# Self-attention of one transformer block: a new step order for units 1 to 14, with small shifts per engine

## The chip, the cores and the metric

One NeuronCore of a Trainium2 chip runs the whole program in a single launch. The metric is device time in microseconds, the median of several runs. Three runs of the kernel before gave 1282.04 us as median (1281.49 to 1285.37).

## What is computed

The input `x` is (2, 1024, 256) in float32. The block adds self-attention, cross-attention, a gated feed-forward and a ternary-weight feed-forward with quantised activations. The change touches the self-attention alone:

```python
h1 = adaln(x, t, norm1_w, norm1_b)
x = mha(h1, h1, attn1_wq, attn1_wk, attn1_wv, attn1_wo, attn1_bo) + x     # 16 heads of 64, 1024 queries and keys
h2 = adaln(x, t, norm2_w, norm2_b)
x = mha(h2, context, attn2_wq, ...) + x                                   # 77 keys
# mha: softmax(q k^T / 8) v per head, then @ wo + bo
```

Matrix products run as sums of fp16 parts: each operand is split into a high part and a low remainder.

## The kernel before, in words

**Units.** Self-attention is done in 16 units (g = 0 to 15), each two heads of one batch. A unit has 16 chunks (c = 0 to 15): head (c // 8), half of the queries (c // 4 % 2), and a group of 256 keys (c % 4). Python code builds one list of steps (`Schedule.attention`, `unit`, `extras`), and each engine gets the same list, from which it runs its own part. The order of the list is therefore the order of work on every engine, except for small shifts (`program`): a step kind may be moved some places up or down on one engine. Before the change such shifts hold for cross-attention only.

**Steps**, with the short names that this document uses:

- S c, `scores` (L797 to L814): four matmuls of 512 columns into one of two PSUM buffers. ACT takes the exponential of the chunk (L1116) into a ring of four SBUF buffers. S c waits until the exponential of chunk c-2 is done.
- R c, `rest`: the low remainder of the exponentials, on Pool (L1406), or on DVE (L1640) for chunks 0, 5 and 11 (`rest_on_pool`, L106).
- V c, `values` (L816 to L839): 24 matmuls of 65 or 64 columns, which need R c. After every fourth chunk DVE divides by the sum (L1651, L1653).
- M, `max`: one matmul of 512 columns (L774) and a DVE maximum over it (L1617). They are numbered by head, tile and key half (M160 is head 1, tile 6, half 0), 32 for a unit, in two PSUM banks by turns, so an M waits for the DVE maximum of the M two places before. The last of each head (M071, M171) also makes the head's negated maximum (L1628). All 16 of head 0 and the first 8 of head 1 are run in the unit before.
- row0, row1: PE transposes the negated maxima of a head (L783), ACT copies them (L1098) and starts a 2 KB DMA from its own queue (L1100) into the operand buffer. S 0 waits for the DMA of row0, S 8 for that of row1.
- q0, q1, k0, k1: projections for the next unit (L753, six matmuls), then ACT (L1087), then DVE (L1602). After k1 the SP queue starts six DMAs (`restack`, L620) that bring them to the layout of the next unit, 1.5 MB in all. The first M of the next unit, M000, waits for the first three.
- v0, v1: value projections (L763, 24 matmuls), ACT (L1091), DVE (L1609).
- out0, out1: transposes of the finished half heads (L787), then ACT (L1106) and DVE (L1633).
- P, `proj`: output projection of an older unit (L730, 12 matmuls), then DVE (L1662). N, `normT`: transposes of normalised tokens (L716), then two DVE operations (L1592). Units 1 to 3 have two N each, units 4 to 7 and 12 to 14 two P, units 8 to 11 two P (with statistics, L1507 and L1511) and two N. Below they are the early, the plain and the double units.

q, k, v, out, P and N share one PSUM bank, so each of them waits on PE until DVE has read the one before (`st.after`):

```python
            def piece(st):
                if st.after:
                    pe.wait_ge(*consumed(st.after))
```

**What sets the order.** In `unit` a loop over the chunks puts S c+1, R c, half of that chunk's other steps, V c-1, the other half, and then `extras` (P and N). Every engine executes its own instructions strictly in the order written, each after its semaphore waits.

## Time and profile before

| | |
|---|---|
| median of three runs | 1282.04 us |
| the profiled execution, its own time | 1283.78 us |
| its span | 1282.0 us |
| PE busy | 1132.9 us (88%) |
| DVE busy | 893.1 us (70%) |
| Pool busy | 640.2 us (50%) |
| ACT busy | 595.1 us (46%) |
| mean granted PE clock | 0.965 |
| share of the chain that ended last | PE 58%, DVE 17%, DMA 9%, issue 5%, ACT 4% |
| start of unit 1's S 1 to start of unit 15's S 1 | 115.44 to 790.40 us |

A busy time is the sum of an engine's instructions. Matmuls overlap in the pipeline (a 512-column matmul lasts 0.38 us and the next starts 0.22 us later), so PE at 88% says little on its own. The time of a step on PE is read from starts, and a wait is where two starts lie further apart than usual.

### The profile page before, as it was taken

To read this page: it belongs to the slowest core of one execution; us is meant where nothing else is said; L and a number is where in the kernel's file an instruction comes from. 1 tells how busy PE (TensorE), PEld (TensorE's weight loads), DVE (VectorE), ACT (ScalarE), POOL (GpSimd) and SP (SyncE) were. 2 spreads that over 40 slices of the span, in tenths; PEclk is the share of its full clock that TensorE was granted. 3 is DMA by queue.
4 is the path that set the end of the run, shared out by engine and by line. 5 is a ranking of instruction groups with operands and counts; after the bars stand their busy time and mean duration, and the time that the engine had idled before them with its cause. 6 is when DMAs were issued, how large, how long until landed. Compare 5 with 4: busy or idle time off the path is not lost.

```text
span 1282.0 us, 30609 instructions
## 1 busy us (share of the span) xinstructions
PE 1132.9 (88%) x12739; PEld 736.9 (57%) x12739; DVE 893.1 (70%) x1754; ACT 595.1 (46%) x855; POOL 640.2 (50%) x572
## 2 busy tenths in 40 slices
PE   4789999999999999899889998988998799799876
PEld 1245655665665665565556655666676566365554
DVE  5668867766766767767757668578688656765764
ACT  3334545444444444444444455445444442465655
POOL 6646755655555555655645555356356343511220
PEclk7799999999999999999999999999999999999987
DMA  7330220121021021020120222134333520000000
GB/s 268 80 85 2 51 51 12 40 51 35 18 51 37 16 51 29 23 51 9 43 51 2 51 51 67 28 81 120 81 70 66 150 85 1 1 5 13 17 2 33
DMA packets 41854, 63.52 MB, mean 50 GB/s; under 512 B 11459, under 2 KB 22383, under 8 KB 41461
## 3 DMA queue, kind: packets, MB, share of 16 engines
q1 hardware_dynamic: 40413, 60.91, 19.0%
q8 instruction: 101, 1.65, 0.5%
q10 hardware_dynamic: 1304, 0.66, 0.2%
q14 instruction: 36, 0.29, 0.1%
HBM read 20.63 MB, written 2.10 MB: 18 GB/s over the span
## 4 chain that ended last, share of the span: by engine, by line
PE 58%; DVE 17%; DMA 9%; issue 5%; ACT 4%; POOL 3%; SPq 3%; DVEq 0%; ACTq 0%
PE outs L753 8%; PE mixed L774 6%; PE scores L812 6%; PE scores L813 6%; DMA head_operands<-qk_pairs 4%; PE scores L871 4%; PE outs L730 4%; PE outs L835 4%; PE outs L837 4%; PE outs L836 3%; DVE maxes L1617 3%; SPq L620 3%; PE outs L887 3%; DMA head_operands<-neg_max_rows 2%; PE outs L763 2%
## 5 line engine op out<-in xcount | busy, mean ns | idle before, releaser
L1406 POOL TENSOR_TENSOR exps_rest<-exps 128x1024 f16<-128x1024 f32 (+1 forms) x267 | 465.2, 1748 | 343.1 <-ACT exps L1116 342.2
L1116 ACT ACTIVATE exps<-scores 128x1024 f32<-128x1024 f32 (+1 forms) x320 | 298.2, 937 | 237.7 <-PE scores L813 226.6
L1617 DVE TENSOR_REDUCE maxes<-mixed 128x1 f32<-128x512 f32 x512 | 335.6, 683 | 62.0 <-PE mixed L774 59.6
L835 PE MATMUL outs<-values,exps 128*128 128x65 f16 (+1 forms) x2176 | 228.4, 193 | 7.3 <-POOL exps_rest L1406 6.8
L812 PE MATMUL scores<-head_operands 128*128 128x512 f16 (+1 forms) x576 | 219.9, 382 | 15.2 <-DMA head_operands<-neg_max_rows 14.8
L836 PE MATMUL outs<-values,exps 128*128 128x64 f16 (+1 forms) x2176 | 228.4, 192 | 0.0
L837 PE MATMUL outs<-values,exps_rest 128*128 128x65 f16 (+1 forms) x2176 | 228.2, 194 | 0.0
L835 PEld LDWEIGHTS outs<-values,exps 128*128 128x128 bf16 (+1 forms) x2176 | 201.7, 98 | 36.0 <-POOL exps_rest L1406 11.1
L813 PE MATMUL scores<-head_operands 128*128 128x512 f16 (+1 forms) x576 | 219.4, 381 | 0.0
L836 PEld LDWEIGHTS outs<-values,exps 128*128 128x128 bf16 (+1 forms) x2176 | 200.8, 98 | 25.9 <-issue 0.3
L774 PE MATMUL mixed<-head_operands 128*128 128x512 f16 x512 | 180.8, 388 | 25.9 <-DMA head_operands<-qk_pairs 11.7
L837 PEld LDWEIGHTS outs<-values,exps_rest 128*128 128x128 f16 (+1 forms) x2176 | 200.8, 97 | 0.0
L753 PE MATMUL outs<-hT,weights 128*128 128x512 f16 x492 | 124.4, 391 | 4.2 <-DVE qk_pairs L1602 1.8
L1602 DVE SCALAR_TENSOR_TENSOR qk_pairs<-outs,qk_pairs 128x512 f16<-128x512 f32 x82 | 56.4, 688 | 94.9 <-ACT qk_pairs L1087 94.9
L774 PEld LDWEIGHTS mixed<-head_operands 128*128 128x128 f16 x512 | 49.9, 98 | 88.0 <-DVE maxes L1617 28.4
L1087 ACT ACTIVATE qk_pairs<-outs 128x512 f16<-128x512 f32 x82 | 49.0, 597 | 105.5 <-PE outs L753 105.5
L812 PEld LDWEIGHTS scores<-head_operands 128*128 128x128 f16 (+1 forms) x576 | 57.8, 100 | 58.7 <-issue 16.9
L730 PE MATMUL outs<-weights,attn_outT 128*128 128x256 f16 x744 | 91.2, 273 | 0.0
L871 PE MATMUL scores<-hT,weights 128*128 128x512 f16 x384 | 90.0, 387 | 1.3 <-DVE exps L1700 1.3
L813 PEld LDWEIGHTS scores<-head_operands 128*128 128x128 f16 (+1 forms) x576 | 58.1, 101 | 50.0 <-issue 1.4
L753 PEld LDWEIGHTS outs<-hT,weights 128*128 128x128 f16 x492 | 44.7, 100 | 57.3 <-DVE attn_outT L1633 9.8
L730 PEld LDWEIGHTS outs<-weights,attn_outT 128*128 128x128 f16 x744 | 70.6, 98 | 11.1
...
## 6 DMA issues: line engine op xcount, KB each, us to landing
head_operands<-qk_pairs SPq DMA_DIRECT2D x128, 256.0 KB, 4.1
...
```

Of the source, the lines that this page charges most:

```text
L730: last = mm(ITEM[bank][:, 0:D], OT[:, c, xh, t * P:(t + 1) * P], W[:, 3, wh, c * D:(c + 1) * D], start=(n_ == 0 and c == 4 * half), stop=( ...
L753: last = mm(m[:, 0:rhs.shape[-1]], W[:, 0 if kind == "q" else 1, wh, wc[c]], rhs, start=(n_ == 0 and c == 0), stop=(n_ == 2 and c == KC - 1))
L774: last = mm(m[:, :], hb[:, QS, t * P:(t + 1) * P], hb[:, KH, kh * HALF:(kh + 1) * HALF], start=True, stop=True)
L812: mm(o, kb[:, KH, :], hb[:, QS, :], start=True, stop=False)
L813: last = mm(o, kb[:, KL, :], hb[:, QM, :], start=False, stop=True)
L835: mm(o, eb[:, sl], vb[:, DH:VW], start=(kt == 0 and q == 0), stop=False, skip_group_check=True)
L836: mm(o[:, 0:DH], eb[:, sl], vb[:, 0:DH], start=False, stop=False, skip_group_check=True)
L837: last = mm(o, R[0:a.ks, slot, sl], vb[:, DH:VW], start=False, stop=(kt == a.kt - 1), skip_group_check=True)
L871: last = mm(SP_[f % 2][:, half * HALF:(half + 1) * HALF], WU[:, wh, k, half * F + f * P:half * F + (f + 1) * P], hT[:, xh, k, tc * HALF:(t ...
L1116: A(E[0:a.ks, c % RING, 0:n], SP_[c % 2][0:a.ks, 0:n], ACT.Exp, scale=SCALE).then_inc(s.exps, 1)
L1406: G.tensor_tensor(R[0:a.ks, c % RING, 0:n], e, e.bitcast(BF16).rearrange("p (n two) -> p n two", two=2)[:, :, 1], ALU.subtract).then_inc(s ...
L1617: V.tensor_reduce(mx[:, h, t, kh:kh + 1], m[:, :], AX_X, ALU.max).then_inc(s.maxed, 1)
```

## The change

Units 1 to 14 no longer come from the loop but from a written table, `SELF_UNIT`. It holds the same steps as before; only their places differ. Units 0 and 15 keep the loop. Besides, `program` now applies shifts in self-attention too, units 0 and 15 included: on Pool P moves 5 steps down and the bias addition 2 up; on ACT the exponentials move 1 up and row 1 down; on DVE the remainders (R) move 4 up. Which remainders run on DVE stays (0, 5, 11).

```diff
+SELF_UNIT = (
+    ("scores", 1), ("rest", 0), ("max", 0, 1, 8), ("max", 0, 1, 9), ("q", 1, 0), ("max", 0, 1, 10), ("slot", 0),
...
+SELF_LAGS = {"POOL": {"proj": 5, "norm": -2},
+             "ACT": {"scores": -1, "row": 1},
+             "DVE": {"rest": -4}}
+SELF_RESTS = (0, 5, 11)
...
-            return c not in (0, 5, 11) if g < UNITS - 1 else bool(c % 2)
+            return c not in SELF_RESTS if g < UNITS - 1 else bool(c % 2)
...
+    def self_unit(self, a, g):
+
+        stage = g // 4
+        pieces = {0: ("norm1", "normT1", "hi1", "lo1"), 2: ("projB", "norm", "normT", "hi", "lo")}.get(stage, ("projA",))
+        for kind, *at in SELF_UNIT:
+            if kind in ("scores", "rest", "values"):
+                self.add(kind, 0, g + at[0] // a.chunks, c=at[0] % a.chunks)
+            elif kind == "slot":
+                self.notes(g, at[0])
+            elif kind in ("q", "k", "v", "row", "out", "max"):
+                what = (kind, at[1]) if kind != "max" else ("max", at[1], at[2] // 2, at[2] % 2)
+                self.add("item", 0, g + at[0], what)
+            elif kind in pieces:
...
         for g in range(UNITS):
-            self.unit(a, g, slots if g else first)
+            if g in (0, UNITS - 1):
+                self.unit(a, g, slots if g else first)
+            else:
+                self.self_unit(a, g)
...
-        lags = LAGS.get(engine, {})
-        at = self.cross_at
+        lags = SELF_LAGS.get(engine, {}), LAGS.get(engine, {})
+        at = self.self_at, self.cross_at
...
-            return i + (lags.get(kind, 0) if i >= at else 0)
+            return i + (lags[1].get(kind, 0) if i >= at[1] else lags[0].get(kind, 0) if i >= at[0] else 0)
```

The order on PE in a plain unit, before and after, in short names (what changed place is easiest seen around V, M and S):

```
before: S1 M M q0 S2 M V0 q1 S3 M M V1 k0 S4 M V2 k1 S5 M V3 M S6 row1 V4 v0 S7 M000 V5 M S8 M M V6 v1 S9 M M V7 M
        S10 M V8 M P S11 M M V9 M S12 M V10 M P S13 M V11 M S14 M row0 V12 M S15 M M V13 out0 S0 M V14 M V15 M M out1
after:  S1 M M q0 M S2 V0 q1 S3 M V1 k0 M S4 M k1 V2 S5 S6 M M S7 V3 row1 v0 V4 V5 M000 M V6 S8 M M v1 S9 M M V7 P M
        S10 M V8 M S11 M M V9 M S12 M P M V10 M V11 S13 M S14 M row0 V12 M S15 V13 M M out0 S0 M V14 M V15 M M out1
```

**DVE at the boundary of two units**, from the division after V 15 to q0's part. L1617 is M, L1633 out1, L1640 R 0, L1602 q0. Before:

```order
L1651 RECIPROCAL rden<-outs 128x4
L1653 TENSOR_TENSOR attn_out<-outs,rden 128x4x64
L1617 TENSOR_REDUCE maxes<-mixed 128x1 x2
L1633 TENSOR_TENSOR attn_outT<-outs,attn_outT 128x512
L1640 TENSOR_TENSOR exps_rest<-exps 128x1024
L1617 TENSOR_REDUCE maxes<-mixed 128x1 x2
L1602 SCALAR_TENSOR_TENSOR qk_pairs<-outs,qk_pairs 128x512
```

The same place after the change (L1670 is M, L1686 out1, L1693 R 0, L1655 q0):

```order
L1704 RECIPROCAL rden<-outs 128x4
L1706 TENSOR_TENSOR attn_out<-outs,rden 128x4x64
L1670 TENSOR_REDUCE maxes<-mixed 128x1
L1693 TENSOR_TENSOR exps_rest<-exps 128x1024
L1670 TENSOR_REDUCE maxes<-mixed 128x1
L1686 TENSOR_TENSOR attn_outT<-outs,attn_outT 128x512
L1670 TENSOR_REDUCE maxes<-mixed 128x1 x2
L1655 SCALAR_TENSOR_TENSOR qk_pairs<-outs,qk_pairs 128x512
```

R 0 has moved ahead of the last M of this group (M131) and of out1.

**DVE around row1**, from k1's part (L1602, L1655) to v0's (L1609, L1662). L1628 and L1681 make the negated maximum that row1 needs. Before:

```order
L1602 SCALAR_TENSOR_TENSOR qk_pairs<-outs,qk_pairs 128x512
L1617 TENSOR_REDUCE maxes<-mixed 128x1
L1651 RECIPROCAL rden<-outs 128x4
L1653 TENSOR_TENSOR attn_out<-outs,rden 128x4x64
L1617 TENSOR_REDUCE maxes<-mixed 128x1
L1628 TENSOR_REDUCE neg_max<-maxes 128x8
L1640 TENSOR_TENSOR exps_rest<-exps 128x1024
L1609 SCALAR_TENSOR_TENSOR values<-outs,values 128x8x64
```

After:

```order
L1655 SCALAR_TENSOR_TENSOR qk_pairs<-outs,qk_pairs 128x512
L1693 TENSOR_TENSOR exps_rest<-exps 128x1024
L1670 TENSOR_REDUCE maxes<-mixed 128x1 x2
L1681 TENSOR_REDUCE neg_max<-maxes 128x8
L1704 RECIPROCAL rden<-outs 128x4
L1706 TENSOR_TENSOR attn_out<-outs,rden 128x4x64
L1662 SCALAR_TENSOR_TENSOR values<-outs,values 128x8x64
```

R 5 now stands ahead of both last maxima (M170, M171) and of the negated maximum; before it stood behind them.

**PE from k0 to k1.** L753 and L806 are the projections, L812 and L813 (L865 and L866) S 4, L774 (L827) an M; where lines are left out stand the 24 matmuls of V 2. Before:

```order
L753 MATMUL outs<-hT,weights 128x512 x6
L812 MATMUL scores<-head_operands 128x512
L813 MATMUL scores<-head_operands 128x512
L812 MATMUL scores<-head_operands 128x512
L813 MATMUL scores<-head_operands 128x512
L774 MATMUL mixed<-head_operands 128x512
...
L753 MATMUL outs<-hT,weights 128x512 x6
```

After:

```order
L806 MATMUL outs<-hT,weights 128x512 x6
L827 MATMUL mixed<-head_operands 128x512
L865 MATMUL scores<-head_operands 128x512
L866 MATMUL scores<-head_operands 128x512
L865 MATMUL scores<-head_operands 128x512
L866 MATMUL scores<-head_operands 128x512
L827 MATMUL mixed<-head_operands 128x512
L806 MATMUL outs<-hT,weights 128x512 x6
```

V 2 has left the space between k0 and k1; it follows k1 now, and an M came in.

## Rows read from the trace of the kernel before

**Rows 1.** Windows, unit 5: span, busy of PE, PEld, DVE, ACT, Pool, PE clock

```profile
300.46:347.70 47.24, 45.08 (x588) 29.28 (x586) 32.26 (x56) 21.46 (x26) 25.28 (x13) 1.00 0.16 35
```

**Rows 2.** Waits of PE, 115.44 to 790.40: total us, times, longest

```profile
PE mixed L783 <- DVE neg_max L1628: 13.0, 24, 1.5
PE mixed L774 <- DMA head_operands<-qk_pairs: 11.0, 11, 2.1
PE scores L812 <- DMA head_operands<-neg_max_rows: 5.9, 4, 1.8
PE outs L835 <- POOL exps_rest L1406: 5.6, 12, 0.6
```

**Rows 3.** Timeline of PE in unit 6: start us, duration us, instruction

```profile
357.87 0.38 PE L774 MATMUL mixed<-head_operands 128*128 128x512 f16 x1
358.09 0.19 PE L835 MATMUL outs<-values,exps 128*128 128x65 f16 x1
358.82 1.46 PE L753 MATMUL outs<-hT,weights 128*128 128x512 f16 x6
360.11 0.38 PE L812 MATMUL scores<-head_operands 128*128 128x512 f16 x1
```

**Rows 4.** Timeline of DVE in unit 6 around k1 and row1

```profile
360.94 0.69 DVE L1602 SCALAR_TENSOR_TENSOR qk_pairs<-outs,qk_pairs 128x512 f16<-128x512 f32 x1 [1.81 <-ACT qk_pairs L1087]
...
362.69 0.68 DVE L1617 TENSOR_REDUCE maxes<-mixed 128x1 f32<-128x512 f32 x1
363.48 0.17 DVE L1628 TENSOR_REDUCE neg_max<-maxes 128x8 f32<-128x16 f32 x1
```

**Rows 5.** Timeline of ACT in unit 6: S 5's exponential, row1

```profile
361.18 1.02 ACT L1116 ACTIVATE exps<-scores 128x1024 f32<-128x1024 f32 x1 [0.27 <-PE scores L813]
...
364.12 0.25 ACT L1098 ACTIVATE neg_max_rows<-mixed 8x128 f16<-8x128 f32 x1
```

**Rows 6.** Timeline of DVE at the boundary of units 5 and 6

```profile
347.01 1.28 DVE L1617 TENSOR_REDUCE maxes<-mixed 128x1 f32<-128x512 f32 x2
348.53 0.69 DVE L1633 TENSOR_TENSOR attn_outT<-outs,attn_outT 128x512 f16<-128x512 f32 x1 [0.25 <-ACT attn_outT L1106]
349.14 1.21 DVE L1640 TENSOR_TENSOR exps_rest<-exps 128x1024 f16<-128x1024 f32 x1
350.27 1.28 DVE L1617 TENSOR_REDUCE maxes<-mixed 128x1 f32<-128x512 f32 x2
```

**Rows 7.** Chain that ended last, at q0 of unit 6: start us, us, what

```profile
349.28 0.39 PE outs L753
```

**Rows 8.** Chain that ended last, units 6 and 7: the restack's DMA

```profile
362.94 5.88 DMA head_operands<-qk_pairs
368.82 0.14 issue
...
411.50 4.75 DMA head_operands<-qk_pairs
```

**Rows 9.** Unit 8: k1's part on DVE (timeline), row1's DMA (chain)

```profile
456.91 0.69 DVE L1602 SCALAR_TENSOR_TENSOR qk_pairs<-outs,qk_pairs 128x512 f16<-128x512 f32 x1 [1.81 <-ACT qk_pairs L1087]
...
461.68 4.40 DMA head_operands<-neg_max_rows
```

**Rows 10.** Timeline of PE in unit 6: M071 and row0

```profile
386.62 0.38 PE L774 MATMUL mixed<-head_operands 128*128 128x512 f16 x1
...
388.48 0.27 PE L783 MATMUL mixed<-identf,neg_max 128*8 128x128 f32 x1 [0.41 <-DVE neg_max L1628]
```

**Rows 11.** Timeline of DVE in unit 8: N, M, P with statistics, R 11

```profile
473.36 0.72 DVE L1592 TENSOR_SCALAR h_full<-outs,norm_cols 128x128 f32<-128x128 f32 x2
...
475.73 0.42 DVE L1662 SCALAR_TENSOR_TENSOR residual<-outs,residual 128x256 f32<-128x256 f32 x1 [0.46 <-PE outs L730]
...
476.81 1.29 DVE L1617 TENSOR_REDUCE maxes<-mixed 128x1 f32<-128x512 f32 x2
...
478.61 2.07 DVE L1640 TENSOR_TENSOR exps_rest<-exps 128x1024 f16<-128x1024 f32 x1
```

More of the change, by code:

```diff
@@ L54 @@
 Q_HI, Q_LO, K_HI, K_LO = range(4)
+SELF_UNIT = (
+    ("scores", 1), ("rest", 0), ("max", 0, 1, 8), ("max", 0, 1, 9), ("q", 1, 0), ("max", 0, 1, 10), ("slot", 0),
+    ("rest", 1), ("scores", 2), ("rest", 2), ("values", 0), ("q", 1, 1), ("scores", 3), ("max", 0, 1, 11),
+    ("slot", 1), ("slot", 2), ("slot", 3), ("values", 1), ("k", 1, 0), ("max", 0, 1, 12), ("scores", 4),
+    ("rest", 3), ("max", 0, 1, 13), ("k", 1, 1), ("values", 2), ("scores", 5), ("scores", 6), ("rest", 4),
+    ("rest", 5), ("max", 0, 1, 14), ("norm1", 0), ("max", 0, 1, 15), ("projB", 0), ("scores", 7), ("rest", 6),
+    ("values", 3), ("row", 0, 1), ("v", 1, 0), ("slot", 4), ("slot", 5), ("values", 4), ("values", 5),
+    ("max", 1, 0, 0), ("max", 1, 0, 1), ("normT1", 0), ("slot", 6), ("values", 6), ("scores", 8), ("rest", 7),
+    ("max", 1, 0, 2), ("norm", 0), ("hi1", 0), ("max", 1, 0, 3), ("v", 1, 1), ("scores", 9), ("rest", 8),
+    ("max", 1, 0, 4), ("max", 1, 0, 5), ("values", 7), ("projA", 0), ("normT", 0), ("slot", 7),
+    ("max", 1, 0, 6), ("slot", 8), ("lo1", 0), ("norm1", 1), ("hi", 0), ("scores", 10), ("max", 1, 0, 7),
+    ("values", 8), ("rest", 9), ("lo", 0), ("max", 1, 0, 8), ("scores", 11), ("rest", 10), ("max", 1, 0, 9),
+    ("hi1", 1), ("max", 1, 0, 10), ("projB", 1), ("slot", 9), ("values", 9), ("normT1", 1), ("max", 1, 0, 11),
+    ("scores", 12), ("slot", 10), ("rest", 11), ("max", 1, 0, 12), ("projA", 1), ("max", 1, 0, 13),
+    ("slot", 11), ("lo1", 1), ("values", 10), ("norm", 1), ("max", 1, 0, 14), ("rest", 12), ("values", 11),
+    ("normT", 1), ("scores", 13), ("hi", 1), ("slot", 12), ("max", 1, 0, 15), ("scores", 14), ("slot", 13),
+    ("rest", 13), ("max", 1, 1, 0), ("row", 1, 0), ("values", 12), ("max", 1, 1, 1), ("lo", 1), ("rest", 14),
+    ("scores", 15), ("values", 13), ("rest", 15), ("max", 1, 1, 2), ("max", 1, 1, 3), ("slot", 14),
+    ("out", 0, 0), ("scores", 16), ("max", 1, 1, 4), ("values", 14), ("max", 1, 1, 5), ("values", 15),
+    ("max", 1, 1, 6), ("max", 1, 1, 7), ("slot", 15), ("out", 0, 1), ("slot", 16))
+SELF_LAGS = {"POOL": {"proj": 5, "norm": -2},
+             "ACT": {"scores": -1, "row": 1},
+             "DVE": {"rest": -4}}
+SELF_RESTS = (0, 5, 11)
 CROSS_UNIT = (
@@ L170, in extras @@
                             self.norm(kind, NT + tile + t)
-            if (g, c) in ((0, 2), (1, 2)):
-                self.add("setup", what="tokens8" if g == 0 else "tokens12")
-            if g == 1 and c in (2, 4, 6, 8):
-                self.add("split_low", what=c // 2 - 1, c=3)
-            if (g, c) in ((14, 8), (14, 11), (15, 1)):
-                self.add("split", c={8: 4, 11: 5, 1: 6}[c])
+            self.notes(g, c)
             if late:
@@ L179, in extras, with notes @@
                     self.add("item", 1, v, what)
+    def notes(self, g, c):
+        if (g, c) in ((0, 2), (1, 2)):
+            self.add("setup", what="tokens8" if g == 0 else "tokens12")
+        if g == 1 and c in (2, 4, 6, 8):
+            self.add("split_low", what=c // 2 - 1, c=3)
+        if (g, c) in ((14, 8), (14, 11), (15, 1)):
+            self.add("split", c={8: 4, 11: 5, 1: 6}[c])
+    def self_unit(self, a, g):
[10 more added lines that the diff above has]
+            elif kind in pieces:
+                tile = 2 * (g % 4) + at[0]
+                if kind[:4] == "proj":
+                    self.proj(0, g // 8 if kind == "projA" else 0, int(kind == "projB"), tile)
+                elif stage == 0:
+                    self.norm(kind if kind == "norm1" else kind[:-1], TPB + tile)
+                else:
+                    self.norm(kind, NT + tile)
     def cross_unit(self, a, g, first_max):
```

2 lines of the change are left out of this document (added).

## The prediction, made before the changed kernel was run

> **What bounds the kernel now.** I read the table first, then the windows of single units, then PE's waits over units 1 to 14, and last the timelines of PE, DVE and ACT around each wait. Unit 5 takes 47.24 us at full clock, and PE is busy for 45.08 of them, DVE for 32.26, ACT for 21.46 and Pool for 25.28 [rows 1]. PE sets the pace, and only where it waits is there anything to win or lose. The waits view names four reasons [rows 2]: the negated maxima for row0 and row1 (13.0 us), the restack's DMA before M000 (11.0), row1's DMA before S 8 (5.9), and remainders on Pool (5.6). An order that lost all four would win 35.5 us.
>
> Steps on PE, from starts [rows 3]: M 0.22, V 0.73 (358.09 to 358.82), q or k 1.29, S (four matmuls like M's) 0.86, v 1.3 (24 matmuls of a quarter of 512 columns), P 1.3 (12 of half), N 0.2, row 0.1. A result is visible 0.21 after its PE step: the exponential of S 5 starts 1.07 after S 5 [rows 3, 5], and 1.07 less 0.86 is 0.21. On DVE an M follows an M after 0.60 (1.28 less 0.68), an operation that follows R starts 1.13 after R's start [rows 6], and the negated maximum is ready 0.96 after the start of its last M [rows 4], for PE 0.14 later [rows 8].
>
> **The change, wait by wait.** No instruction is added or removed, so the price is only in waits.
>
> *q0, all 14 units: +11.3.* At the unit's boundary DVE starts M130 at 347.01 and M131 at 347.61, ends out1's part at 349.22, and q0, which needs the bank, starts at 349.28 [rows 6, 7]. Now R 0 stands between the two M. Its exponential is ready in time: S 0 starts 0.86 + 0.22 + 0.73 + 0.22 + 0.73 = 2.76 before M130's matmul and needs 1.07 + 1.02. So R 0 starts at 347.61, M131 at 348.74, out1's part at 349.34, which ends at 350.03, and q0 starts at 350.09: 0.81 later. In the old place R 0 stood behind out1, where PE waited for nothing of it. If DVE had slack there the cost would be 0; at most it is the whole 1.13.
>
> *k1, 14 units: +3.9.* k1 needs k0's bank. From start to free a projection takes 2.87 (358.82 to 360.94, 0.69, and 0.06 as at q0) [rows 3, 4, 7]. Between them PE now has k0, M, S, M = 2.59, without V 2's 0.73. It waits 0.28. Before it did not wait.
>
> *row1, early and plain units: +4.4.* Count from S 5's start. Its exponential ends at 2.09, R 5 starts at 2.15 and now stands ahead of M170: M170 3.28, M171 3.88, negated maximum 4.84, row1 at 4.98. PE arrives after S 5, S 6, M, M, S 7, V 3 = 3.75 and waits 1.23. Before, the maximum ended at 363.65 [rows 4] and row1 could go at 363.79, while PE had finished S 6 at 360.11 + 0.86 + 0.22 + 0.73 + 0.22 + 0.86 = 363.00, so it waited 0.79. That is +0.44 in each of ten units. In the double units a P of 1.3 covers both.
>
> *M000: -10.4.* In the new order k1 starts 2.02 before S 5, its DVE part ends 2.81 after its start, so at +0.79. In unit 6 the first three DMAs were there 7.3 us after this point, in unit 7 6.2 (1.3 to the third issue, 5.88 or 4.75, 0.14) [rows 8]. PE now arrives at M000 after row1's 4.98 + 0.1 + 1.3 (v0) + 1.46 (V 4, V 5) = 7.84, which is 7.05 after it. The 11.0 us of [rows 2] go; of the long kind (three units) 0.2 stays each.
>
> *S 8: +2.9.* What is late next is row1's own DMA, since R 5 has delayed row1 and V 6 is all that came between. ACT copies it from 5.31 to 5.56 (0.33 after row1, 0.25 long) [rows 5], that is 4.8 after k1's part. In unit 8 the copy was done at 461.66, 4.1 after k1's part (457.60), and the row was there at 466.22: 4.54 after the copy, 8.6 after k1's part [rows 9]. PE arrives at S 8 at 7.84 + 0.44 + 0.73 = 9.01, or 8.2 after k1's part. If the row lands no earlier than in unit 8 the wait is 0.4, if it again takes 4.54 it is 1.1. I take 0.6, nearer to the first, because by then the restack's six DMAs are nearly through. In the double units ACT first does S 7's exponential, which needs V 3 (end 5.06); the copy ends at 6.55, 5.8 after k1's part, PE arrives at 8.3: 0.3 to 2.0, taken as 0.7. Ten times 0.6 and four times 0.7 is 8.8, and the 5.9 of [rows 2] go.
>
> The Trainium skill (DMA: Bandwidth & Descriptors, Queues, rings and completion order) says that a DMA engine goes round its queues packet by packet, so a 2 KB row would not stand behind 1.5 MB. By it S 8 would not wait at all; the trace's 4.40 us for such a row [rows 9] speaks against it. It is a rival below.
>
> *row0: -4.0.* Before, a division stood ahead of M071, and row0 came 1.86 after M071's matmul [rows 10] with 1.30 of work between: 0.56 of waiting. Now S 13 stands between V 11 and M071, so row0 can go 0.22 + 0.21 + 0.96 + 0.14 = 1.53 after it, a wait of 0.23. That is 0.33 in ten units, and I take half of it in the double ones, where N mixes in.
>
> *M061, early units: +4.3.* R 11 and N now stand ahead of M051 on DVE. From S 11's start: R 11 starts at 2.49 (behind M041 at 1.29 and M050 at 1.89), N at 3.62, M051 at 4.25 (N takes 0.63 [rows 11]); its bank is free at 4.99. PE arrives at M061 after S, M, M, V, N, M, S, M = 3.55 and waits 1.44, in three units. *Double units: +4.5.* There P's DVE part (1.08 from 475.73 to 476.81 [rows 11]) starts at 2.8, R 11 at 3.9, M051 at 5.0, free at 5.77; PE arrives at 4.64 and waits 1.13, in four units. In the plain units P's 1.3 lies between and covers it.
>
> *Remainders on Pool: -4.0.* The twelve waits of 5.6 us are three in each double unit [rows 2]. Pool now does R 10 ahead of P's statistics (shift 5), and the first two should go; the third, before V 15, behind N's part, I leave at 0.4. Bounds: -5.6 and 0.
>
> At no cost: the shift of ACT's exponentials (exponentials and rows keep their turns except ahead of row1, counted above), the 2 up of Pool's bias additions (nobody waits for them [rows 2]), and units 0 and 15, where R moves ahead of q1 and P on DVE: an exponential is ready 2.1 after its S, before those are. If that cover fails, eight R of 1.13 in unit 15 cost some 3 us; if V 8 to V 10 come sooner, they win 1.
>
> In unit 8 an R on DVE took 2.07 instead of 1.21 while Pool did its own [rows 6, 11]. The Trainium skill (SBUF — State Buffer, Who interferes with whom) explains it: a DVE instruction with two SBUF inputs and a Pool instruction share a port that is held for a whole instruction. By it R 0 and R 5 at their new places cost nothing more, as Pool's R 15 and R 4 end before them; were one caught, each catch would add up to 0.9.
>
> **Sum.** 11.3 + 3.9 + 4.4 - 10.4 + 2.9 - 4.0 + 4.3 + 4.5 - 4.0 = +12.9 us. The profiled execution took 1283.78 us, 1.74 above the median of the runs, so 1296.7 for its like and 1295 for the median.
>
> **Rivals.**
> - *The rows of maxima wait for the whole restack (slower still).* Then S 8 waits 1.1 and 2.0: 10 x 0.5 + 4 x 1.3 = +10, 1305 us. For it: the 4.54 of unit 8. Against: the traffic is older when the row is issued.
> - *The rows slip in between (near no change).* S 8 never waits: -8.8, 1286 us. For it: only four units ever waited there. Against: [rows 9].
> - *The moved remainders cost nothing (faster).* DVE is idle for 15 us of a unit [rows 1]. If R 0, R 5 and R 11 fell into such gaps, q0, row1 and both M061 terms were nil: 12.9 - 11.3 - 4.4 - 4.3 - 4.5 = -11.6, 1270 us. It decides at one place: whether DVE starts out1's part as soon as ACT has done its own. Against: DVE takes its work in written order, and around M130 it has no gap [rows 6].
>
> **How the numbers follow.** Forecast 0.58 (its own range 1288 to 1302), rows late 0.14, rows early 0.13, remainders free 0.15. A measurement of this kernel can tell about 0.3% (3.8 us) from no change, so faster is under 1278.2 and slower over 1285.9. Faster 0.13 is nearly all of the last case. Same 0.13 is the rest of it and most of the rows-early case. Slower 0.74 is what is left. The range 1276 to 1307 takes the rows-late case in and cuts off most of the free remainders; the long DMAs, which fell in three units, can fall in none or in six (some 4 us), and lie inside it.
>
> **What would show it.** In the changed profile PE's wait for out1's DVE part before q0 should be near 1.1 in each unit (0.3 before), M000 should hardly wait, row1 should wait for L1681 by about 1.2 with R 5 on DVE just before M170, S 8 should wait for the row's DMA in nearly every unit, and M061 in seven. A plain unit should last 47.24 + 0.81 + 0.28 + 0.44 - 0.8 + 0.6 - 0.33, about 48.2. I am wrong if a plain unit lasts less than 47.2, or if DVE runs R 0 without delaying out1.

## The result and the profile after

| | before | changed |
|---|---|---|
| median, us (runs) | 1284.96 (13) | 1292.91 (13) |
| lowest to highest | 1276.72 to 1292.38 | 1287.65 to 1299.83 |
| profiled execution, its span | 1283.78, 1282.0 | 1299.83, 1298.0 |
| S 1 of unit 1 to S 1 of unit 15 | 674.96 | 684.47 |
| unit 15 | 46.81 | 43.18 |

The changed kernel takes 1.0069 times as long, 95% interval 1.0043 to 1.0096, or +8.9 us (5.5 to 12.3); the two medians lie 8.0 us apart. The forecast was 1295 us, slower. The profiled execution of the changed kernel is the longest of its 13, so its whole span overstates the change. Its start (66.25 us to S 1 of unit 0, 61.28 before) and what follows unit 15 (448.9 after 444.8) account for that. The kernels below all leave both alone, and there the two ranged from 60.7 to 66.9 and from 440.5 to 446.6. So I compare the units.

The head of the page after:

```profile
span 1298.0 us, 30602 instructions
PE 1138.3 (88%) x12732; PEld 739.2 (57%) x12739; DVE 890.8 (69%) x1754; ACT 594.4 (46%) x855; POOL 626.5 (48%) x572
```

Windows of the changed kernel, unit 5 (the answer to [rows 1]) and unit 15 (span, busy PE, PEld, DVE, ACT, Pool, clock):

```profile
313.03:360.93 47.90, 45.23 (x589) 29.44 (x587) 32.47 (x56) 21.46 (x26) 24.65 (x13) 1.00 0.15 35
805.92:849.10 43.18, 38.81 (x547) 25.80 (x545) 26.93 (x44) 21.72 (x28) 16.33 (x8) 0.99 0.19 39
```

The plain unit is 0.66 longer with the same work on every engine, so only waits can have changed. Unit 15 of the kernel before:

```profile
790.40:837.21 46.81, 39.47 (x547) 26.10 (x545) 28.40 (x44) 21.74 (x28) 16.99 (x8) 0.96 0.16 34
```

Its clock differs too: the mean granted clock of unit 15 was 0.96 before and 0.99 after.

PE's waits in the changed kernel over the middle units, 121.46 to 805.92 (total us, times, longest), against [rows 2]:

```profile
PE mixed L827 <- DVE maxes L1670: 16.8, 24, 1.7
PE mixed L836 <- DVE neg_max L1681: 11.6, 11, 1.1
PE scores L865 <- DMA head_operands<-neg_max_rows: 8.3, 11, 2.0
...
PE outs L806 <- DVE attn_outT L1686: 2.9, 14, 0.2
PE outs L888 <- POOL exps_rest L1459: 1.3, 4, 0.3
...
PE mixed L827 <- DMA head_operands<-qk_pairs: 0.2, 1, 0.2
```

M000's wait is gone (11.0 to 0.2), eight of the twelve on Pool too (5.6 to 1.3). New are 16.8 us in which an M waits for a DVE maximum. All but three of the 24 stand at two places, M141 and M061.

At the boundary of a unit, DVE and then PE (start us, us, instruction), against [rows 6, 7]:

```profile
360.23 0.68 DVE L1670 TENSOR_REDUCE maxes<-mixed 128x1 f32<-128x512 f32 x1
360.83 1.22 DVE L1693 TENSOR_TENSOR exps_rest<-exps 128x1024 f16<-128x1024 f32 x1
361.96 0.69 DVE L1670 TENSOR_REDUCE maxes<-mixed 128x1 f32<-128x512 f32 x1
362.56 0.68 DVE L1686 TENSOR_TENSOR attn_outT<-outs,attn_outT 128x512 f16<-128x512 f32 x1
```

```profile
362.70 0.39 PE L827 MATMUL mixed<-head_operands 128*128 128x512 f16 x1 [0.54 <-DVE maxes L1670]
363.30 0.39 PE L806 MATMUL outs<-hT,weights 128*128 128x512 f16 x1 [0.21 <-DVE attn_outT L1686]
```

R 0 stands between M130's maximum and M131's, and from M130's maximum to q0 it is 3.07 us, where it was 2.27. The wait is split: 0.70 of it falls on M141, which needs M131's bank, and 0.38 on q0 (0.28 before).

In a double unit, behind P's DVE part and R 11:

```profile
491.02 0.42 DVE L1715 SCALAR_TENSOR_TENSOR residual<-outs,residual 128x256 f32<-128x256 f32 x1 [0.24 <-PE outs L783]
...
492.04 1.19 DVE L1693 TENSOR_TENSOR exps_rest<-exps 128x1024 f16<-128x1024 f32 x1
493.15 1.28 DVE L1670 TENSOR_REDUCE maxes<-mixed 128x1 f32<-128x512 f32 x2
```

```profile
493.90 0.39 PE L827 MATMUL mixed<-head_operands 128*128 128x512 f16 x1 [0.89 <-DVE maxes L1670]
```

The chain that ended last, from S 5 to S 8 of unit 6 (start us, us, what), against [rows 4, 5, 9]:

```profile
375.50 1.03 ACT exps L1169
376.55 1.23 DVE exps_rest L1693
377.78 1.21 DVE maxes L1670 x2
...
379.08 0.18 DVE neg_max L1681
379.26 0.14 issue
379.40 0.28 PE mixed L836
...
380.00 3.71 DMA head_operands<-neg_max_rows
383.71 0.14 issue
383.84 0.38 PE scores L865
```

R 5 delays the last two maxima of head 1, these delay row1, and the row's DMA then ends PE's wait at S 8.

**The terms.** For each step of PE I took the time to the next start and subtracted the usual pace of that step, the same in both kernels (S 0.861 us, V 0.730, q and k 1.292, v 1.337, P 1.308, out 0.436, N 0.217, M 0.215, row 0.107). What is left is waiting, or time at a lower granted clock. Summed over units 1 to 14, us:

| wait at | forecast change | before | after | change |
|---|---|---|---|---|
| q0, and M141 ahead of it | +11.3 | 4.0 | 15.2 | +11.2 |
| k1 | +3.9 | 0 | 4.9 | +4.9 |
| row1 | +4.4 | 8.8 | 12.2 | +3.4 |
| M000 | -10.4 | 13.6 | 0.6 | -13.0 |
| S 8 | +2.9 | 4.7 | 10.6 | +5.9 |
| row0 | -4.0 | 8.1 | 4.4 | -3.7 |
| M061 | +8.8 | 0.1 | 8.9 | +8.8 |
| V 10, V 12 (Pool) | -4.0 | 5.1 | 0.4 | -4.8 |
| all others | 0 | 21.0 | 17.8 | -3.2 |
| sum | +12.9 | 65.4 | 75.0 | +9.6 |

The middle stretch itself grew by 9.5, so the waits account for all of it: without them a plain unit takes 44.09 before and 44.05 after. In "all others" the largest changes are S 0 (-2.4, nearly all one wait of the kernel before in unit 11), M030 (-1.5), M070 and V 9 (-0.6 each), and against them M040 (+1.0) and M041 (+0.7). With unit 15's -3.6 and unit 0's +1.0 (54.16 to 55.20) the change up to the end of unit 15 is +6.9; the medians differ by 8.0.

Each kernel also lost some 1.7 us to the clock once, right behind PE's longest wait of this stretch. In the changed kernel S 8 of unit 10 waited 2.20, and from 581.97 to 585.39 the granted clock was 0.50 (1.2 GHz; the same columns as above):

```profile
581.97:585.39 3.42, 3.42 (x25) 2.60 (x24) 1.61 (x3) 1.02 (x1) 1.30 (x2) 0.50 0.00 0
```

In it v1 took 2.40 us instead of 1.34. In the kernel before M000 of unit 12 waited 2.24, and the clock was 0.50 from 665.52 to 668.93. So what looks like a wait behind v1 in unit 10 is PE at work at the lower level.

### The profile page after: what moved, and what is told of

Same layout as the page of the kernel before. It is cut to its first block, busy times and chain, and to the rows that moved or that the text cites. A ratio compares the mean times of both kernels' runs of the same rounds, so it can differ in the third digit from the quotient of the medians.

```text
span 1298.0 us, 30602 instructions
## 1 busy us (share of the span) xinstructions
PE 1138.3 (88%) x12732; PEld 739.2 (57%) x12739; DVE 890.8 (69%) x1754; ACT 594.4 (46%) x855; POOL 626.5 (48%) x572
## 4 chain that ended last, share of the span: by engine, by line
PE 56%; DVE 21%; DMA 7%; issue 5%; ACT 5%; POOL 3%; SPq 3%; DVEq 0%; ACTq 0%
PE outs L806 8%; PE scores L865 6%; PE scores L866 6%; PE mixed L827 5%; DVE maxes L1670 5%; DMA head_operands<-neg_max_rows 4%; PE scores L924 4%; PE outs L783 4%; PE outs L890 3%; PE outs L888 3%; PE outs L889 3%; DVE exps_rest L1693 3%; SPq L673 3%; PE outs L940 2%; PE outs L816 2%
## 5 line engine op out<-in xcount | busy, mean ns | idle before, releaser
L1459 POOL TENSOR_TENSOR exps_rest<-exps 128x1024 f16<-128x1024 f32 (+1 forms) x267 | 456.5, 1716 | 369.9 <-ACT exps L1169 369.8
L1670 DVE TENSOR_REDUCE maxes<-mixed 128x1 f32<-128x512 f32 x512 | 336.5, 685 | 77.4 <-PE mixed L827 73.9
L865 PE MATMUL scores<-head_operands 128*128 128x512 f16 (+1 forms) x576 | 220.4, 383 | 20.8 <-DMA head_operands<-neg_max_rows 17.5
L866 PE MATMUL scores<-head_operands 128*128 128x512 f16 (+1 forms) x576 | 220.4, 383 | 0.0
L827 PE MATMUL mixed<-head_operands 128*128 128x512 f16 x512 | 181.8, 390 | 28.4 <-DVE maxes L1670 22.7
L806 PE MATMUL outs<-hT,weights 128*128 128x512 f16 x492 | 125.4, 393 | 8.5 <-DVE attn_outT L1686 4.0
L1655 DVE SCALAR_TENSOR_TENSOR qk_pairs<-outs,qk_pairs 128x512 f16<-128x512 f32 x82 | 56.6, 691 | 103.5 <-ACT qk_pairs L1140 103.5
L827 PEld LDWEIGHTS mixed<-head_operands 128*128 128x128 f16 x512 | 48.0, 98 | 88.9 <-DVE maxes L1670 48.7
L865 PEld LDWEIGHTS scores<-head_operands 128*128 128x128 f16 (+1 forms) x576 | 57.9, 101 | 68.7 <-issue 19.5
L866 PEld LDWEIGHTS scores<-head_operands 128*128 128x128 f16 (+1 forms) x576 | 58.2, 101 | 49.4 <-issue 1.2
L806 PEld LDWEIGHTS outs<-hT,weights 128*128 128x128 f16 x492 | 44.8, 100 | 67.1 <-DVE qk_pairs L1655 12.4
L1693 DVE TENSOR_TENSOR exps_rest<-exps 128x1024 f16<-128x1024 f32 x53 | 65.2, 1230 | 25.0 <-ACT exps L1169 25.0
```

The source lines that it names most:

```text
L806: last = mm(m[:, 0:rhs.shape[-1]], W[:, 0 if kind == "q" else 1, wh, wc[c]], rhs, start=(n_ == 0 and c == 0), stop=(n_ == 2 and c == KC - 1))
L827: last = mm(m[:, :], hb[:, QS, t * P:(t + 1) * P], hb[:, KH, kh * HALF:(kh + 1) * HALF], start=True, stop=True)
L865: mm(o, kb[:, KH, :], hb[:, QS, :], start=True, stop=False)
L866: last = mm(o, kb[:, KL, :], hb[:, QM, :], start=False, stop=True)
L1459: G.tensor_tensor(R[0:a.ks, c % RING, 0:n], e, e.bitcast(BF16).rearrange("p (n two) -> p n two", two=2)[:, :, 1], ALU.subtract).then_inc(s ...
L1670: V.tensor_reduce(mx[:, h, t, kh:kh + 1], m[:, :], AX_X, ALU.max).then_inc(s.maxed, 1)
```

## The experiments

Each is one edit. "Plain unit" is unit 5 or the span over units 4 to 7, in the kernel's profiled execution. Unless said otherwise the edit is to the changed kernel, and ratios are to the kernel before.

### 1. R 0 back behind out1

```diff
 # in place(): DVE's R 0 of units 1 to 14 gets no shift
+            if engine == "DVE" and kind == "rest" and st.ai == 0 and st.c == 0 and 0 < st.g < UNITS - 1:
+                return i
```

> The changed kernel, but R 0 of units 1 to 14 keeps its old place on DVE, behind out1 and ahead of M140. Theory (remainders ahead of maxima on DVE make PE wait): PE's waits before M141 and q0, 0.70 and 0.40 in the changed kernel, shrink to the 0.3 before q0 of the kernel before, so a unit is 0.8 us shorter (a plain unit 47.1 instead of 47.9) and the program about 11 us faster than the changed kernel, 0.2% faster than the kernel before. Rival (the loss is in the order of PE's steps and the DMA of the row of maxima, whatever DVE does): R 0 moves nothing, a plain unit stays at 47.9.

Measured: 1286.49 us, ratio 1.0016 (0.9993 to 1.0040), against the changed kernel's 1.0069 (1.0043 to 1.0096). Plain unit 47.50 to 47.58 (unit 7 48.14). M141's 0.70 is gone and q0 is back at 0.28, as the term says. But another wait has come, on PE behind q0 (start us, us, instruction):

```profile
361.29 1.47 PE L808 MATMUL outs<-hT,weights 128*128 128x512 f16 x6
363.02 0.39 PE L829 MATMUL mixed<-head_operands 128*128 128x512 f16 x1 [0.26 <-DVE maxes L1672]
```

This is M150. In the new order it follows q0 at once, and it needs the bank of M140, whose maximum DVE reaches only after R 0, at 362.28. It waits 0.44 against the pace, so of the 0.80 a unit only 0.36 is won. In the kernel before no M waited behind q0, with R 0 in this same place.

### 2 and 3. The shifts alone, and the order alone

```diff
 # 2: old order, new shifts
-            if g in (0, UNITS - 1):
-                self.unit(a, g, slots if g else first)
-            else:
-                self.self_unit(a, g)
+            self.unit(a, g, slots if g else first)
```

> The old order of steps in all units, with the new shifts per engine (R 4 up on DVE, P 5 down and bias 2 up on Pool, exponentials 1 up and row 1 down on ACT). Theory: R 0 ahead of M131 costs 0.8 before q0, R 5 ahead of the last maximum costs row1 1.2 of which M000's wait of 0.8 swallows a part, R 11 ahead of M051 costs M061 0.4: some 1.9 us per unit, 1310 us (+2%). Rival (the shifts are harmless, the written order is what costs): within 0.3% of the kernel before.

```diff
 # 3: new order, no shifts
+SELF_LAGS = {}
```

> The new order of steps with all shifts of self-attention at zero. Theory: the waits before M141 and q0 shrink by 0.8 in 14 units, those before M061 (1.4 in three early units, 1.05 in four double ones) go, since R 11 is behind M051 again; row1's 1.2 stays, since the table itself puts R 5 ahead of M170; the waits on Pool's remainders in the double units come back in part. About 18 us faster than the changed kernel, 1275 us, 0.8% faster than the kernel before. Rival (order costs, shifts harmless): as slow as the changed kernel, about 1293.

Measured: the shifts alone 1299.09 us, ratio 1.0136 (1.0096 to 1.0176); the order alone 1286.19 us, 1.0021 (1.0003 to 1.0039). So most of the loss comes with the shifts. That it is DVE's remainders among them is read from the waits of these kernels and from experiments 1 and 4; no run moves DVE's alone. The shifts alone had been expected to take 1310; but M000's wait, 13.6 before, fell to 0.8, and unit 15 became 4.2 shorter. In the old order the shifts cost more than in the new: with R 5 ahead of the last maximum row1 waits 2.03 a unit (23.3 us over the fourteen, 12.2 in the changed kernel), which the waits of that kernel show (total us, times, longest):

```profile
PE mixed L833 <- DVE neg_max L1678: 26.5, 28, 2.3
PE scores L862 <- DMA head_operands<-neg_max_rows: 8.9, 9, 1.5
PE mixed L824 <- DVE maxes L1667: 8.1, 16, 0.5
```

Without shifts row1 still waits 12.2, since the table itself puts R 5 ahead of M170: that term comes with the order. And three wins that I had counted on stayed away (1275 expected). R 0 back in its place makes M150 wait 0.44, as in experiment 1, 6.2 us in all. R 11, back in its place, no longer delays M061 (but for 0.36 in the early units) but M070 behind it (5.1 us in all, 0.70 in a double unit):

```profile
486.75 0.39 PE L825 MATMUL mixed<-head_operands 128*128 128x512 f16 x1 [0.54 <-DVE maxes L1668]
```

And unit 15 took 46.77 there, 42.64 with the shifts alone: what makes unit 15 shorter is the shift, not the order. DVE in unit 15 of the kernel before, then Pool:

```profile
795.61 2.29 DVE L1500 SCALAR_TENSOR_TENSOR weights<-stage,weights 128x2048 f16<-128x2048 f32 x1 [0.77 <-ACT weights L1044]
797.82 2.92 DVE L1640 TENSOR_TENSOR exps_rest<-exps 128x1024 f16<-128x1024 f32 x1
```

```profile
796.83 2.83 POOL L1406 TENSOR_TENSOR exps_rest<-exps 128x1024 f16<-128x1024 f32 x1 [2.02 <-ACT exps L1116]
```

And DVE in unit 15 of the changed kernel:

```profile
810.05 1.23 DVE L1693 TENSOR_TENSOR exps_rest<-exps 128x1024 f16<-128x1024 f32 x1
811.84 2.29 DVE L1553 SCALAR_TENSOR_TENSOR weights<-stage,weights 128x2048 f16<-128x2048 f32 x1 [0.57 <-ACT weights L1097]
```

R 2 stood behind the split of a weight (2.29 us) and beside Pool's R 3, where it took 2.92, and the maxima behind it let PE wait 2.38 at M161:

```profile
801.40 0.39 PE L774 MATMUL mixed<-head_operands 128*128 128x512 f16 x1 [2.38 <-DVE maxes L1617]
```

Four places up it is ahead of the split, alone, and takes 1.23: the remainder ends 5.13 after the split's start before, and 0.56 ahead of it now. Besides, the granted clock of the kernel before was 0.50 for 3.41 us from 802.05, right behind that wait, and q1 took 2.54 us from 802.60 instead of 1.29: part of the 3.6 is the clock.

### 4. All remainders of units 0 to 14 on Pool

```diff
-SELF_RESTS = (0, 5, 11)
+SELF_RESTS = ()
```

> The changed kernel with the remainders 0, 5 and 11 of units 0 to 14 on Pool too, none on DVE (SELF_RESTS empty). Theory: the waits before M141 and q0 fall to 0.3, row1's 1.2 to about 0.1, those before M061 go; row1's copy on ACT then stands behind the exponential of S 7, so S 8 waits for the row's DMA by about 1.5 instead of 0.6. A plain unit 46.3, the program about 20 us faster than the changed kernel, near 1273. Rival (Pool becomes the bound: 16 remainders of 1.9 are 30 us of a unit of 47, and in the double units and early units Pool has 4 to 8 us more): V 1, V 6 and V 12 wait for Pool by over 1 us each and nothing is won.

Measured: 1266.51 us, ratio 0.9879 (0.9848 to 0.9911). Plain unit 46.9 to 47.0 (unit 7 47.8). M141's wait is gone, row1's is 0.1, M061's is 0.36 in the early units only. Pool, busy for 30.1 of a unit's 46.9, isn't late anywhere new. With the divided remainders out of the way, most of what PE still waits for is row1's DMA (total us, times, longest; the next line is out1's wait for the division, which all kernels have):

```profile
PE scores L865 <- DMA head_operands<-neg_max_rows: 14.5, 13, 1.9
PE outs L840 <- DVE attn_out L1706: 5.4, 14, 0.4
PE mixed L827 <- DMA head_operands<-qk_pairs: 2.9, 4, 1.3
```

This confirms the three terms that rest on a remainder on DVE: over the fourteen units q0 with M141 fell by 11.2, row1 by 11.2 and M061 by 7.8. Of these 30.2 us S 8 took 6.0 back and M000, which PE now reaches earlier, 3.6. So S 8 isn't late only because row1 is: the copy now ends 4.39 after k1's part instead of 4.75, and S 8 still goes no sooner than 8.5 after it, so that PE, which is there earlier, waits longer (1.2 to 1.5 in the plain units, 2.05 once).

### 5. R 5 behind the negated maximum

```diff
 # in place(): DVE's R 5 of units 1 to 14 goes behind M171 and its negated maximum
+            if engine == "DVE" and kind == "rest" and st.ai == 0 and st.c == 5 and 0 < st.g < UNITS - 1:
+                return i + (3.5 if st.g < 4 else 2.5)
```

> The changed kernel, but R 5 of units 1 to 14 stands on DVE behind M171 and its negated maximum instead of ahead of M170. Theory: row1's wait of 1.2 in ten units falls to about 0.1; its copy on ACT then stands behind the exponential of S 7, so the copy comes only 0.4 earlier against k1 and S 8's wait grows from 0.5 to about 1.4. Net 0.3 to 0.4 less for a plain unit (47.5 instead of 47.9), nothing in the double ones; the program 3 us faster than the changed kernel, within its noise. Rival (what follows row1 is not late, so removing its wait pays in full): a plain unit 46.7, the program 11 us faster.

Measured: 1290.58 us, ratio 1.0038 (1.0014 to 1.0063). Plain unit 47.75 to 47.8 (unit 7 48.6). The time is near what I expected for another reason. Row1's wait went, and S 8's nearly so (10.6 to 3.0 over the fourteen units); what took their place is V 4, which needs the division after V 3 (12.3 us in the early and plain units), and in the double units v0, which waits 1.1 to 1.3 for P's part on DVE (5.1 us in all). DVE, and PE at V 4:

```profile
374.96 0.17 DVE L1683 TENSOR_REDUCE neg_max<-maxes 128x8 f32<-128x16 f32 x1
375.04 2.43 DVE L1695 TENSOR_TENSOR exps_rest<-exps 128x1024 f16<-128x1024 f32 x1
377.39 0.17 DVE L1706 RECIPROCAL rden<-outs 128x4 f32<-128x4 f32 x1
377.60 0.42 DVE L1708 TENSOR_TENSOR attn_out<-outs,rden 128x256 f32<-128x256 f32 x1
```

```profile
378.17 0.19 PE L890 MATMUL outs<-values,exps 128*128 128x65 f16 x1 [1.29 <-DVE attn_out L1708]
```

Pool did its own remainders at that time:

```profile
374.50 4.73 POOL L1461 TENSOR_TENSOR exps_rest<-exps 128x1024 f16<-128x1024 f32 x2 [2.42 <-ACT exps L1171]
```

R 5 took 2.43 where it took 1.23 at its place in the changed kernel. In each such pair of these traces it is the operation that started second that was lengthened: R 5 here, R 2 in unit 15 before, and Pool's R 1 in experiment 1 (2.24, behind an R 0 of 1.21). The Trainium skill (SBUF — State Buffer, Who interferes with whom) tells of a port that such a DVE instruction and a Pool instruction hold by turns; the trace agrees as far as it goes: 2.43, 2.92 and [rows 11] 2.07 where one of Pool's remainders had started before, 1.19 to 1.23 where DVE was alone or first. No run here takes Pool's alone away at one of these places.

### 6. Head 1's restack behind row1's DMA

All remainders on Pool as in 4, and in units 1 to 14 SP issues the second three DMAs of the restack only when row1 of the unit has landed:

```diff
+                    if ai == 0 and h == 1 and 1 < g:
+                        sp.wait_ge(s.rows[1], 16 * g + CREDIT)
```

> The kernel with all remainders on Pool, and in restack the three DMAs of the second head (h = 1) wait until row1's DMA of the unit before has landed (SP waits for rows[1]; units 2 to 15). Theory (the 2 KB row is late because 1.5 MB of restack is on the same DMA engines): the row lands some 2.7 us after its copy instead of 4.2, S 8's wait of 1.2 to 1.5 falls to under 0.3 in 13 units, nobody waits for the second head's operands (needed 17 us later); 15 us faster than the kernel with all remainders on Pool, 1251. Rival (the row's time is its own latency, whatever else moves, as packet-wise turns between queues would have it): S 8 waits as before, 1266.

Measured: 1248.04 us, ratio 0.9707 (0.9664 to 0.9751), 18.5 us under 4. Plain unit 45.51, a window of it:

```profile
292.76:338.28 45.52, 44.82 (x589) 29.35 (x587) 29.38 (x53) 21.36 (x26) 30.14 (x16) 1.00 0.17 37
```

S 8 waits once in the fourteen units (0.9, in unit 10). When row1's copy ends on ACT and when the restack of head 1 starts, which needs the row there:

```profile
355.91 0.25 ACT L1153 ACTIVATE neg_max_rows<-mixed 8x128 f16<-8x128 f32 x1
```

```profile
357.87 1.95 SPq L675 DMA_DIRECT2D head_operands<-qk_pairs  x3
```

From the end of the copy, 356.16, to 357.87 are 1.71 us, the most that the row can have taken, for the same 2 KB that took 3.71 in the changed kernel. The DMA packets say where the time went. Here head 0's packets had ended at 357.09, and the row's ran alone, from 357.47 to 357.55. In unit 6 of the changed kernel they ran from 382.22 to 382.83, in the midst of the restack's, and the row landed another 0.88 later. So what makes the row late is the restack's traffic, not the DMA's own time.

### 7. Row1 ahead of the exponential of S 7

All remainders on Pool, and on ACT:

```diff
+            if engine == "ACT" and kind == "scores" and st.ai == 0 and st.c == 7 and 0 < st.g < UNITS - 1:
+                return i + 3.5
+            if engine == "ACT" and st.ai == 0 and st.what == ("row", 1) and 0 < st.g < UNITS - 1:
+                return i
```

> The kernel with all remainders on Pool, and on ACT row1's copy and DMA stand ahead of the exponential of S 7 in units 1 to 14. Theory: the copy ends 0.8 earlier (0.8 to 0.9 in the double units), but under the restack's traffic the row lands only 0.3 to 0.8 earlier; S 8 waits 0.4 to 0.8 less, 6 to 10 us faster than the kernel with all remainders on Pool, about 1259. Rival (S 8's release is set by the end of the restack, 8.6 us after k1's part, whenever the row is issued): no change, 1266.

Measured: 1255.39 us, ratio 0.9759 (0.9720 to 0.9797), 11.1 under 4. Plain unit 45.8 to 46.8, S 8's waits fell from 16.6 to 4.3. The row's copy ends 3.64 after k1's part instead of 4.39, and in four of the seven plain units S 8 goes 7.4 to 7.5 after it, with hardly a wait. In units 5 and 7 it still waits 1.1.

### 8. The old order with all remainders on Pool

The edits of 2 and 4 together.

> The old order of steps in all units, with the new shifts, and no remainders of units 0 to 14 on DVE. It tells whether the 18 us that the kernel with all remainders on Pool wins over the kernel before come from the new order or from the division. Theory (the remainders at their old places on DVE cost nothing, the new order wins once they are gone): plain units as before, 47.2, unit 15 shorter by 3.6 as in the changed kernel; about 1280. Rival (the division alone wins): 1266.

Measured: 1275.02 us, ratio 0.9917 (0.9884 to 0.9951). The old order keeps row1's 0.80, M000's 0.8 to 2.1 and row0's 0.57. Against 4 the new order is 8.5 us faster, once it is rid of the remainders on DVE. I had expected 1280 and had not counted on V 10 and V 12, which wait 0.8 us in all here and 5.1 in the kernel before.

### 9. V 2 back between k0 and k1

```diff
-    ("rest", 3), ("max", 0, 1, 13), ("k", 1, 1), ("values", 2), ("scores", 5), ("scores", 6), ("rest", 4),
+    ("rest", 3), ("max", 0, 1, 13), ("values", 2), ("k", 1, 1), ("scores", 5), ("scores", 6), ("rest", 4),
```

> The changed kernel with V 2 back between k0 and k1 on PE. It isolates the term k1 (+0.28 a unit forecast; 0.30 measured as a wait of PE for k0's bank). Theory A, the term is real time: k1 no longer waits and a unit is 0.3 shorter, 14 units, 4 us: ratio 0.9965 to the changed kernel, some 1289 us. Theory B, which I hold (0.7): S 8 is bound by row1's DMA, which is bound by the restack that k1's DVE part starts. k1 now starts 0.43 later, S 5 0.30 earlier, the row is copied 4.0 after k1's part instead of 4.7, and in unit 8 of the kernel before a copy at 4.1 landed 8.6 after it. PE reaches S 8 7.5 after k1's part, so S 8 waits 1.1 instead of 0.4 to 1.0 and gives back what k1 won: 1291 to 1294 us, no measurable change, plain unit 47.7 to 47.9. M000 then has 0.1 of slack instead of 0.8 and may wait 0.1 to 0.3.

Measured: 1295.4 us, ratio 1.0067 (1.0042 to 1.0092): no difference from the changed kernel that the intervals show. K1's wait went from 4.9 to 0.5 over the fourteen units, S 8's rose from 10.6 to 14.7. The row's DMA in unit 6, and S 8:

```profile
375.43 4.53 DMA head_operands<-neg_max_rows
```

```profile
380.10 0.38 PE L865 MATMUL scores<-head_operands 128*128 128x512 f16 x1 [1.04 <-DMA head_operands<-neg_max_rows]
```

S 8 goes 8.71 after k1's part here, and the copy had ended 4.02 after it; in unit 6 of the changed kernel it is 8.62 and 4.75. Over the units and kernels the moment at which S 8 could go hardly depends on when the row is sent, within a stretch:

| copy ends after k1's part | kernel, units | S 8 goes after k1's part |
|---|---|---|
| 3.64 | 7, units 4 and 6 | 7.43 to 7.47 |
| 4.02 to 4.05 | before, units 8, 10, 11; 9, units 4 and 6 | 8.59 to 8.71 |
| 4.39 | 4, units 4 to 6 | 8.54 to 8.62 |
| 4.75 | changed, units 4 to 6 | 8.62 to 8.75 |
| 4.84 to 4.97 | 7 and 9, units 8 to 11 | 8.66 to 8.79 |
| 5.70 | changed, units 9 and 11 | 9.49 to 9.50 |

Left out are unit 7, where it was 9.3 to 9.4 in the changed kernel, 4 and 9 and 8.4 in 7, unit 5 of 7 (8.2), units 8 and 10 of the changed kernel (9.3 and 10.6), and unit 5 of this kernel, where the row came in time for 7.5. The row's packets do run earlier when it is sent earlier: in unit 6 they end 7.19 after k1's part with the copy at 4.39, and 7.61 with it at 4.75. It is between the last packet and S 8 that the time is lost again, 1.39 and 1.01 us. That S 8's moment stays where it is makes k1's gain come back as a wait. M000, which PE reaches 6.4 after k1's part here and 7.1 in the changed kernel, didn't wait.

### 10. Head 1's restack behind row1's DMA, remainders divided as in the changed kernel

> The changed kernel with one wait more on SP: the restack of head 1 is issued when row1 of the same unit has landed, so that the row has the queues to itself but for head 0's three DMAs. Remainders stay divided between DVE and Pool as in the changed kernel. Theory (row1's DMA lies under the restack's traffic): S 8's wait goes, 0.4 to 1.0 in ten units and 1.0 to 2.2 in four, 10 to 12 us: 1281 us. k1 0.30, row1 1.22, M141 0.70, q0 0.40 and M061 stay as they are; a plain unit 47.2. Rival (the row takes 4.4 us by itself): S 8 waits as before and the time is 1293 us or more, since head 1 then comes later.

Measured: 1280.56 us, ratio 0.9973 (0.9947 to 0.9999). Plain unit 47.41 to 47.43, all four alike:

```profile
309.17:356.60 47.43, 45.06 (x589) 29.36 (x587) 32.46 (x56) 21.48 (x26) 24.65 (x13) 1.00 0.16 35
```

S 8's wait is 0 in units 1 to 14, and M141 0.70, row1 1.22, k1 0.28 and M061 stay to the hundredth. S 8 is a term of its own, 10.6 us.

### 11. The same on the old order, remainders on Pool

> The order of the kernel before, with the changed kernel's small shifts per engine, all remainders of units 0 to 14 on Pool and head 1's restack behind row1's DMA. It tells what the new order is worth once Pool has the remainders: the same edit on the new order gave 1248 us, without the restack's edit the old order gave 1275 and the new one 1266. Theory: S 8's 1.4 goes in four units and 0 to 1 in the others, 6 to 10 us: 1267 us. M000's 0.8 to 2.1, row1's 0.8 and row0's 0.57 stay, since V 2 between k0 and k1 and the two V behind row1 are as they were: the old order stays some 18 us slower than the new one. Rival (M000's wait was contention with head 1's DMAs): M000's wait goes too and the old order comes within 5 us of the new one, 1253 us.

Measured: 1266.89 us, ratio 0.9863 (0.9818 to 0.9908). The waits (total us, times, longest):

```profile
PE mixed L835 <- DVE neg_max L1680: 13.1, 25, 1.5
PE mixed L826 <- DMA head_operands<-qk_pairs: 8.4, 11, 2.0
```

Row1, row0 and M000 still wait. Against 8, M000's wait fell by 3.8 of 14.1 us, so some of it was head 1's traffic, but most is the place of M000 in the order. The new order with the same edits (6) is 18.9 us faster. That is what the order is worth, and the changed kernel doesn't show it.

### 12. Edits of 6 and 7 together

> The new order and shifts, all remainders of units 0 to 14 on Pool, head 1's restack behind row1's DMA, and on ACT row1's copy ahead of the exponential of S 7. Each of the last two alone took S 8's wait, 18 and 11 us. If they treat one and the same wait, together they are worth no more than the better alone: 1248 us, plain unit 45.5, S 8 without a wait, and what is left is out1 0.58, q0 0.30, k1 0.30 and row0 0.24. If the copy's place had a gain of its own (ACT or the double units' row1), it would be 1242 to 1245. If the later exponential of S 7 now delays Pool's R 7 and V 7, 1251 or more.

Measured: 1250.40 us, ratio 0.9718 (0.9682 to 0.9754); 6 alone gave 0.9707. Plain unit 45.51 in both. The two remedies treat one wait.

## Why the prediction was right, and where it wasn't

**Q0, +11.3: held (+11.2).** The chain M130, R 0, M131, out1, q0 was 3.07 against the 3.08 worked out (0.60 + 1.13 + 0.60 + 0.69 + 0.06). That 0.70 of it would appear as a wait of M141 and not of q0 I had not seen, since I followed only out1's bank (I had named 1.1 at q0 as the sign; it was 0.38 there); the sum is the same. Experiment 4 takes the remainder away, and the wait with it. What I said beside it, that in the old place R 0 cost nothing, holds for the old order alone: experiment 1 got back 0.36 a unit and not 0.81.

**K1, +3.9: held in each unit but the first** (0.28, as worked out); unit 1 had 1.25, so the sum is +4.9. But experiment 9 shows that it wasn't a price that could be undone: without it S 8 waits as much more.

**Row1, +4.4: held** (+3.4: 1.22 against the 1.23 forecast and 0.80 before in the plain units; unit 1 had had 1.62 before, which I took for 0.79).

**M000, -10.4: held** (-13.0). By PE's pace it had cost 13.6, by the waits view, from which I took it, 11.0. The small waits of 0.2 that I feared for the long DMAs came to 0.6 in all.

**S 8, +2.9: right in place, low in size (+5.9).** Two readings were off. The 5.9 of [rows 2] are not all S 8's: that line holds the DMAs of both rows, and its longest wait, 1.8 at 639.22, is S 0's, for row0. S 8 had waited in units 8, 10 and 11 alone, 4.5 us (and lost 0.2 to the clock). After the change it waited 0.07 to 1.05 in the plain units and 0.2 to 0.9 in the early ones (forecast 0.6), 0.9 to 2.2 in the double ones (0.7). Three of the ten (0.23, 0.30 and 0.07) and one of the four (2.20) lie outside the 0.4 to 1.1 and 0.3 to 2.0 that I had given. In the double units my value had the row there 3.2 us after its copy (5.8 and 9.0 after k1's part); the table under experiment 9 has it at 3.8. From the rule of the Trainium skill (DMA: Bandwidth & Descriptors, Queues, rings and completion order), that a DMA engine goes round its queues packet by packet, I had concluded that S 8 would be free. The runs refute that conclusion, not the rule, which is on the order of packets: the row's packets did run between the restack's, but its landing took 3.71 to 4.53 us in the rows shown, and at most 1.71 when head 1's half was held back.

**Row0, -4.0, and M061, +8.8: held** (-3.7, +8.8; M061 1.43 and 1.05 a unit against 1.44 and 1.13, and 1.88 in unit 1). Experiment 3 adds that M061's wait is the remainder's and would have gone to M070 with the remainder in its old place.

**Remainders on Pool, -4.0: held** (-4.8), and V 15 stayed, as said.

**Units 0 and 15, at no cost: wrong for unit 15, -3.6.** I had asked only what R's earlier place would delay and allowed 1 us of gain. The row that would have told me was there in the trace before, R 2 of 2.92 us behind a weight's split, but I had read no DVE timeline of unit 15. The named terms came to +12.7 of the +12.9; this step and the -3.2 of the steps that I had put at nothing make the real change the smaller one.

**The number.** That 1295 lies so near to 1292.9 is in part luck. I forecast +12.9 on the median of three runs, 1282.04. The medians of thirteen differ by 8.0, and that of the kernel before is 1284.96: a change 4.9 too large stood on a base 2.9 too low. A plain unit was to last 48.2; unit 5 lasted 47.90, since S 8 waited 0.46 and not 0.6, and M030 no longer waited its 0.15.

**The rivals.** "The moved remainders cost nothing" is refuted by 1 and 4: taking them off DVE gives 26 us. "The rows slip in between" is refuted by the changed kernel, where S 8 waits in all of units 1 to 14. "The rows wait for the whole restack" has the right mechanism (6 and 10), but S 8's waits came to 10.6 and not the 19 that it gave (1.1 and 2.0 a unit).

What stays open is why a row sent anywhere between 4.0 and 5.0 us lands at one time (which of the restack's DMAs it waits for isn't in these rows). For the 2.20 at S 8 in unit 10 the packets show what went with it: fourteen of the row's sixteen had run by 579.22, the last two at 579.97 and 580.22, and from 579.07 to 579.99 one DMA engine had a packet of 16 KB of the instruction queue. The same stands behind S 8's one wait in experiment 6 (instruction packet 543.09 to 544.44, the row's last two at 544.42 and 544.45) and behind S 0's in the kernel before (636.61 to 637.91; 637.90 and 637.93), where the row took 3.80 us with no restack under way. No run takes such a packet away, so that it is the cause is not shown.
